# Making the last three of five chunk projections early: a graph transformer kernel on one core

## The reference, cut to what matters

```python
q = (feat @ Wq.T + bq).reshape(n, H, D)              # edge attention
e = jnp.einsum('ehd,ehd->eh', q[src], k[dst]) * scale
m = jax.ops.segment_max(e, dst, num_segments=n)
ex = jnp.exp(e - m[dst])
...
skip = feat @ Wskip.T + bskip
g = jax.nn.sigmoid(jnp.concatenate([skip, rst, skip - rst], axis=-1) @ Wgate.T + bgate)
rst = g * skip + (1.0 - g) * rst
...
return out * gate @ Wproj + bproj                    # the mix branch
...
h = relu(bn(x @ W1[e])); h = relu(bn(h @ W2[e])); y = h @ Wo[e]   # eight experts
```

## Time and profile before

| | |
|---|---|
| median of 3 runs | 3044.85 us (3041.48 to 3045.27) |
| profiled execution, its own time | 3041.24 us |
| span of that execution (first to last instruction) | 3039.0 us |
| mean granted TensorE clock | 0.947 of 2.4 GHz |
| TensorE busy with matmuls | 2647.0 us (87%) |
| VectorE busy | 2047.7 us (67%) |
| ScalarE busy | 1382.4 us (45%) |
| GpSimd busy | 1056.8 us (35%) |

### The profile page before, as it was taken

One profiled execution on the slowest core, in us unless ns is written; L12 is line 12 of the kernel. 1 busy time (PEld: TensorE's weight loads), 2 busy tenths in 40 slices (PEclk: granted clock), 3 DMA queues, 4 the chain that ended last, 5 costly groups with the idle time before them and its releaser, 6 DMA issues. The chain is left out here.

```text
span 3039.0 us, 54927 instructions
## 1 busy us (share of the span) xinstructions
PE 2647.0 (87%) x12024; PEld 2072.3 (68%) x12025; DVE 2047.7 (67%) x4093; ACT 1382.4 (45%) x2916; POOL 1056.8 (35%) x1184
## 2 busy tenths in 40 slices
PE   7777787768994999999998999999979977869698
PEld 6545555455552777777767888888858865647587
DVE  6676777878888553644226888888899968955411
ACT  2214332218882443343333444444489948845122
POOL 1576777732110000000006666666500008810033
PEclk9897999989996999999999999999989989989799
DMA  4699999937774000000017777777601131042353
GB/s 134 220 315 288 292 313 303 321 92 224 230 227 137 6 1 9 9 1 9 1 37 235 214 214 213 214 215 214 202 14 40 49 118 71 1 177 87 96 174 128
DMA packets 236591, 443.79 MB, mean 146 GB/s; under 512 B 29017, under 2 KB 128801, under 8 KB 235068
## 3 DMA queue, kind: packets, MB, share of 16 engines
q1 hardware_dynamic: 179518, 261.89, 27.7%
q0 software_dynamic: 56960, 180.47, 19.0%
HBM read 350.56 MB, written 92.69 MB: 146 GB/s over the span
## 5 line engine op out<-in xcount | busy, mean ns | idle before, releaser
L1889 PE MATMUL bank<-sums 128*128 128x256 f32 x2352 | 542.7, 381 | 2.6 <-issue 2.6
L1965 POOL DMA_INDIRECT conv_h<-table_h,conv_ix x392 | 374.4, 955 | 293.1 <-ACT conv_ix L1936 171.6
L1889 PEld LDWEIGHTS bank<-sums 128*128 128x128 f32 x2352 | 434.6, 191 | 55.3 <-issue 3.0
L1696 ACT ACTIVATE area<-bank,nodes_bi,nodes_sc 128x320 f32<-128x320 f32 x320 | 197.6, 618 | 359.9 <-PE bank L1604 359.9
L714 POOL DMA_INDIRECT x<-table_qv,scores_ix x300 | 286.5, 955 | 187.2 <-ACT scores_ix L618 108.5
L1867 DVE SCALAR_TENSOR_TENSOR x<-bank,nodes_w,x 128x256 f32<-128x256 f32 x200 | 96.4, 484 | 309.4 <-PE bank L1613 309.3
L1424 PE MATMUL bank<-attend_pv,x 128*128 128x260 f32 x800 | 220.0, 403 | 26.7 <-POOL attend_pv L1354 24.6
L734 PE MATMUL bank<-sums,area 128*128 x800 | 230.9, 416 | 11.6 <-issue 6.0
L1424 PEld LDWEIGHTS bank<-attend_pv,x 128*128 128x128 f32 x800 | 137.1, 190 | 109.4 <-issue 62.7
L1936 ACT ACTIVATE conv_ix<-src 128x2 int32 x196 | 39.9, 203 | 359.5 <-DVE conv_msg L1986 347.0
L1986 DVE TENSOR_TENSOR conv_msg<-bank,conv_h 128x512 f32<-128x512 f32 x196 | 135.6, 692 | 95.7 <-PE bank L1889 86.1
(11 more groups left out here) (491 smaller groups left out, 5819.9 us busy)
## 6 DMA issues: line engine op xcount, KB each, us to landing
sums<-in_edges SPq DMA_DIRECT2D x196, 384.0 KB
x<-edge_v SPq DMA_DIRECT2D x200, 256.0 KB, 3.0
edge_v<-x SPq DMA_DIRECT2D x150, 256.0 KB, 4.7
hidden_rows<-top_wide SPq DMA_DIRECT2D x25, 512.0 KB, 3.2
projected<-spline_hst SPq DMA_DIRECT2D x10, 960.0 KB, 4.4
ball_hT<-projected SPq DMA_DIRECT2D x5, 1920.0 KB, 18.0
top_wd<-in_top_wd SPq DMA_DIRECT2D x8, 1024.0 KB
x<-in_x SPq DMA_DIRECT2D x10, 640.0 KB, 8.8
```

What stands on the lines that cost most here:

```text
L1696: nc.scalar.activation((h1, h2)[layer][:, o, hf * CW:(hf + 1) * CW], banks[n % HIDS][:, 0:CW], ACT.Relu, scale=sc[:, layer, e, o:o + 1], b ...
L1889: mm = nc.tensor.matmul(banks[u][:, g * F:(g + 1) * F], m.conv_eT[:, u, g, c], m.conv_w[:, c], start=False, stop=c == EC - 1, skip_group_c ...
L1965: nc.gpsimd.indirect_dma_start(out=h[:, u, g, :], out_offset=None, in_=m.d_h, in_offset=bass.IndirectOffsetOnAxis(ap=ix[:, u * G + g:u * G ...
```

## The change

`EARLY_MIX` goes from 2 to 5, so the Wproj products of all five chunks are fills. The list grows from 19 to 28 fills. Six in place of four stand in the last round of the scores pass, and nine, eight and five in place of seven, five and three beside the scans. In the node layers the condition `p >= EARLY_MIX` is never true any more, so the product behind expert 1 is gone for chunks 2, 3 and 4, and all chunks take L1818.

```diff
-EARLY_MIX = 2
+EARLY_MIX = 5
 EARLY_TILES = ([("skip", t, min(t + 2, NT)) for t in range(0, NT, 2)]
                + [("mix", c * U + u, c * U + min(u + 2, U)) for c in range(EARLY_MIX) for u in range(0, U, 2)])
-EARLY_IN_SCORES = 4
-EARLY_BESIDE_SCANS = (7, 5, 3)
+EARLY_IN_SCORES = 6
+EARLY_BESIDE_SCANS = (9, 8, 5)
```

## The result

The changed kernel took 3036.20 us (median of six runs, 3032.58 to 3037.55), the kernel before 3044.86 (six runs, 3041.48 to 3051.45). The medians differ by 8.7 us. The ratio of the two kernels, estimated from all runs, is 0.9967, with a 95% interval from 0.9956 to 0.9979: 10.0 us less, between 6.4 and 13.4. The forecast was 11.7 less (3033.1). The profiled execution took 3036.58 us, with a span of 3034.9.

The account below looks back on a forecast made before the run. TensorE was taken to bound the node layers, with gaps beside the scans. Removal -12.93 plus +1.20 beside the scans gave -11.7 us, from the median 3044.85 to 3033.1; range 3027.8 to 3038.3.

Parts of the forecast that it names:

- The removal, -12.93: Node layers: three products leave TensorE's queue behind expert 1, 4.31 us each, all of it real gain.
- The twin round: Node layers: the preceding round, chunk 1 already early, where VectorE waits only 0.53 us for expert 2's output.
- What it cost in the node layers, 0: Node layers: no cost in the sum; one 1.2 GHz stretch, 1.7 us, kept either way for the range.
- 4.31 us are gone ahead of them: Node layers' middle rounds: slow-clock stretches may move after the removal; one costs some 1.7 us.
- The fills in the scores pass, 0: Last scores round: two more fills, 3.78 us, end over 5 us before the block's end; cost 0.
- Forward scan, 0: Beside the forward scan: six more matmuls, 2.67 us, end 0.74 us before VectorE's ends; cost 0.
- Before the backward ends, +0.14: Second part beside the scans: 26 matmuls at full clock take 11.65 us, ending 0.14 us late.
- the third part, +1.06: Before the result is turned: 16 matmuls take 7.17 us; with the +0.14 before, 1.20 us later.
- the rival: Beside the scans: clock falls as before in second and third parts, +1.68 and +1.79, giving 3036.6; chance 0.15.
- about half of that idle stretch is filled, and I expect the clock to stay: Before the second part: first part ends 2.67 us later within a 5.20 us near-idle stretch, keeping 2.4 GHz.
- 0.64 against 0.15: Whole kernel: chance of the forecast, 3033.1 us, against that of the clock falling beside the scans, 3036.6.
- The port: Node-layer additions: VectorE's two SBUF inputs don't contend with GpSimd's memset, cost 0; rival 1.7 us back, chance 0.08.

Follow-up runs that it names:

- the fills alone: All 28 fills as in the changed kernel, but the three products still made in the node layers too; 3048.47 us, ratio to before 1.0010.
- second and third profile: The changed kernel profiled twice more, unchanged: 3035.93 and 3029.52 us.
- first profile: The changed kernel's first profiled execution, nothing altered: 3036.58 us.
- full rows: Changed kernel with both operands of the product L1671 filled with zeros from eight to 128 rows; 3036.30 us, ratio to before 0.9974.

## Why the prediction was right, and where its terms were off

**The removal, -12.93.** Right: 4.3 us in each of three rounds (124.0 to 119.7, a costly stretch set aside), with and without the fills, and VectorE's wait at 0.52 us where 0.46 was worked out. The twin round had shown it.

**What it cost in the node layers, 0.** Missed. The forecast kept one stretch of low clock, 1.7 us, either way for the range and none in the sum. Measured: +1.7 in the last round in three profiles of three, and in the first four rounds +1.7, -1.7 and -1.7 against before's one. The last round's 115.2 stands in all nine profiles with eight rows other than the two of before, that with the fills alone included, whose rounds are not shorter. So the forecast's reason for a move, that "4.31 us are gone ahead of them", does not explain this one, and the cause is open.

The price of a stretch was misread as well. The two that the earlier trace rows show, at 1088.80 and 1338.00, cost no time: their rounds take 124.0 us, as a round without a stretch does. Only the third, in the round of 125.6, cost 1.7. A stretch costs half its length where TensorE is last behind it, and not in every place where TensorE is busy.

**The fills in the scores pass, 0.** Right: the last one ends at 627.70 (625.81 + 1.89), and the scans start no later.

**Forward scan, 0.** Right, but closely: 0.56 us left, and 0.05 and 0.02 in the second and third profile, where the first part took 0.5 us more.

**Before the backward ends, +0.14, and the third part, +1.06.** Right in the second and third profile: together +0.9 in the scans where +1.20 was forecast. In the first profile, and in the runs with the fills alone and with full rows, the clock fell as the rival had it for the second part (+1.68; measured 13.18 - 11.49 = 1.69). Its second half, a fall in the third part, was seen in no profile of the changed kernel or with its order of fills. So the step "about half of that idle stretch is filled, and I expect the clock to stay" failed in three of five profiles with this order of fills: 2.1 to 2.8 us of lull were left. 0.64 against 0.15 was too sure.

**The port.** The addition for chunk 4 beside the memset:

```profile
1369.02 1.18 POOL L1572 MEMSET sums<- 128x1300 f32 x1 [29.70 <-DVEq L1815]
1369.06 1.63 DVE L1818 TENSOR_TENSOR x<-x,rows 128x512 f32<-128x512 f32 x3
```

1.63 us, no more than alone, as L130 had it. The rule of the Trainium skill (SBUF — State Buffer, Who interferes with whom), that two SBUF inputs don't contend with a GpSimd instruction that only writes, agrees.

**Sum.** -12.9 in rounds, +1.7 in the last, +0.9 to +2.4 in the scans, and 1.7 more or less for a stretch: -12 to -7, with the measured -10.0 near its middle. In the second and third profile the two stages give -11.8 and -11.9, close to the forecast's -11.7, but that is luck: the last round's +1.7 is offset by before's costly stretch in the third round, which these executions didn't have. In the first profile they give -7.0.

## What to carry to other kernels

Work that is taken off an engine's path saves its full price if the engine that would be last next still has idle time at that very place. Look for a round of the same kernel that already lacks the work: its wait is the answer. Where work goes in front of a small operation that another engine's chain waits for, count it at both clock levels, and see whether the little gaps inside the chain can hold a piece of it. A slow stretch costs only where nothing else is last: read the wait behind it before removing it.

## What the hardware showed that I had not expected

- TensorE's clock fell while TensorE was wholly busy, right behind 2.42 us of matmuls with eight rows of weights. With the same matmuls at 128 rows, 120 of them zeros, no fall came there in two profiles of two kernels: 0 of 8 places, against 34 of 44 with eight rows. The ten took much the same time, 2.42 and 2.32 us.
- The same program is 1.7 us longer or shorter per stretch, in steps: rounds of 119.7 or 121.3 us and nothing between. Three profiles of one kernel gave 662.3, 662.4 and 665.7 us for the node layers. The forecast had cited the Trainium skill (TensorE: Matmul & The Clock Gate, What's actually happening) for such differences between runs, and these profiles agree. What they add is that some places, as the last round, were hit each time.
- Before the second part beside the scans TensorE has only small products to do. The clock fell behind such lulls of 2.77, 2.42 and 2.14 us and stayed behind those of 1.92 and 1.90. With 1.05 us of matmuls put in, it stayed in all three profiles where VectorE was on time. The two short lulls are those before which an earlier stretch of low clock had held up the work longest.
- A stage that nobody touched took between 215.3 and 221.7 us from one execution to the next, more than half of what the change is worth, with a granted clock of 0.91 and 0.89. One run of each kernel would not have been enough to judge it.
